# Third convolution of a four-layer block, written out image by image, with a smaller-of-two similarity in place of a squared-norm product

## The reference, cut to what matters

```python
EPS = 1e-08
xf = x.reshape(b, c, p)                                   # p = 256 places of an image
dots = einsum('bcp,bcq->bpq', xf, xf)
norms = sqrt(sum(xf * xf, axis=1))
denom = maximum(norms[:, :, None] * norms[:, None, :], EPS)
sim = square(relu(dots / denom))
tx = einsum('oc,bcq->boq', W, xf) + bias[None, :, None]
out = einsum('bpq,boq->bop', sim, tx)
```

## Time and profile before

| | |
|---|---|
| median of 3 runs | 1095.7 us (1092.54 to 1098.52) |
| the profiled execution | 1098.47 us, with a span of 1096.7 us |
| busy, share of the span | PE 81%, DVE 52%, ACT 40%, POOL 35% |
| mean granted PE clock | 0.823 of full |
| third convolution | from about 578 us to about 680.7 us |

### The profile page before, as it was taken

How to read it: one execution, slowest core, us unless ns; L and a number is a source line. 1 busy time by engine, 2 the same in 40 slices (tenths; PEclk the granted TensorE clock), 3 DMA queues, 4 the chain that set the end, 5 groups by cost and what they waited for, 6 DMA issues and landing times.

```text
span 1096.7 us, 16813 instructions
## 1 busy us (share of the span) xinstructions
PE 888.8 (81%) x5406; PEld 412.6 (38%) x5406; DVE 574.0 (52%) x1939; ACT 443.7 (40%) x800; POOL 379.8 (35%) x453
## 2 busy tenths in 40 slices
PE   4867777896888988887778877889999988668895
PEld 1222222221555656553225655223333324442221
DVE  6787764543444444534656555356464456344542
ACT  3212114653345454443442223234343334656552
POOL 0343433555323222243440020543534422014532
PEclk9787777998589798895895666899999995788977
DMA  9400002222000000001340000322223200002421
GB/s 180 65 18 8 7 9 80 79 91 66 1 2 2 2 2 2 2 2 59 107 147 0 0 0 16 121 73 85 80 81 91 80 1 0 0 1 78 130 78 66
DMA packets 48629, 52.43 MB, mean 48 GB/s; under 512 B 18774, under 2 KB 27114, under 8 KB 48554
## 3 DMA queue, kind: packets, MB, share of 16 engines
q1 hardware_dynamic: 47530, 50.43, 16.9%
q0 software_dynamic: 1024, 1.05, 0.5%
HBM read 49.75 MB, written 1.70 MB: 47 GB/s over the span
## 4 chain that ended last, share of the span: by engine, by line
PE 60%; DVE 17%; issue 9%; POOL 7%; ACT 4%; DMA 1%; SPq 1%; DVEq 1%; POOLq 0%; ACTq 0%
PE ps L772 16%; PE ps L777 10%; PE ps L1260 5%; PE ps L327 4%; PE ps L1305 3%; PE ps L1613 2%; PE ps L1255 2%; DVE code L475 2%; DVE best L471 2%; PE ps L1232 2%; PE ps L1595 2%; POOL work L1140 2%; PE ps L1586 1%; PE ps L714 1%; POOL frstd L1085 1%
## 5 line engine op out<-in xcount | busy, mean ns | idle before, releaser
L772 PE MATMUL ps<-xT,wall 64*128 64x512 f32 x576 | 172.3, 680 | 7.0 <-ACT work L891 3.3
L777 PE MATMUL ps<-work,down 128*64 128x512 f32 x576 | 164.1, 650 | 9.0 <-POOL work L1128 8.3
L1007 DVE TENSOR_TENSOR work<-aq,ps 128x512 f32<-128x512 f32 x128 | 82.2, 684 | 106.9 <-PE ps L772 105.6
L891 ACT ACTIVATE work<-ps,b1t 128x512 f32<-128x512 f32 x160 | 100.4, 685 | 79.7 <-PE ps L772 79.5
L1121 POOL TENSOR_TENSOR work<-xT,cwb 128x512 f32<-128x512 f32 x64 | 81.4, 1274 | 125.2 <-PE ps L772 97.4
L886 ACT ACTIVATE aq<-ps 128x512 f32<-128x512 f32 x128 | 69.4, 594 | 123.8 <-PE ps L772 123.8
L1140 POOL TENSOR_TENSOR work<-work 128x512 f32<-128x512 f32 x56 | 71.1, 1269 | 87.4 <-DVE work L1033 85.1
L772 PEld LDWEIGHTS ps<-xT,wall 64*128 64x128 f32 x576 | 54.0, 204 | 112.0 <-issue 106.2
L1033 DVE SCALAR_TENSOR_TENSOR work<-ps,b1t,cwb 128x512 f32<-128x512 f32 x64 | 47.9, 748 | 82.8 <-PE ps L777 68.5
L772 PE MATMUL ps<-work,wall 64*128 64x512 f32 x256 | 74.2, 656 | 11.8 <-POOL work L1121 6.5
L777 PEld LDWEIGHTS ps<-work,down 128*64 128x64 f32 x576 | 30.0, 140 | 98.0 <-issue 39.0
(11 more groups left out here) (229 smaller groups left out, 1541.8 us busy)
## 6 DMA issues: line engine op xcount, KB each, us to landing
cwb<-weight_rows SPq DMA_DIRECT2D x320, 128.0 KB, 3.0
wall<-in_L_ffn_w_dram SPq DMA_DIRECT2D x4, 512.0 KB, 10.5
wall<-in_L_ffn_W_dram SPq DMA_DIRECT2D x4, 256.0 KB, 9.5
out_dram<-tokens SPq DMA_DIRECT2D x8, 128.0 KB, 1.7
tokens<-in_x_dram SPq DMA_DIRECT2D x1, 896.0 KB, 5.6
ak<-in_L_conv_emb_dram SPq DMA_DIRECT2D x2, 256.0 KB
down<-in_L_ffn_W_dram SPq DMA_DIRECT2D x2, 256.0 KB
down<-in_L_ffn_w_dram SPq DMA_DIRECT2D x1, 512.0 KB
```

What stands on the lines that cost most here:

```text
L772: ins = pe.matmul(m.ps[:, bank + half, :], m.wall[r, at + g * P:at + (g + 1) * P], x[r, :], start=True, stop=True)
L777: ins = pe.matmul(m.ps[half * C:half * C + C, bank, :], m.down[l][:, n % G, :], m.hid[:, n % 3, half, :], start=start, stop=True, skip_gro ...
L891: act.activation(m.hid[:, n % 3, half, :], m.ps[:, 2 * (n % 2) + half, :], ACT.Gelu, bias=bias)\
L1007: dve.tensor_tensor(m.hid[:, n % 3, half, :], m.silu[:, n % 2, half, :], m.ps[:, 2 + half, :], ALU.mult)\
```

## The change

The loop over pairs becomes slots over images, all written out, in which PE handles image j+2 (transposes), j+1 (dot products), j (linear map) and j-1 (outputs). The norm moves from DVE to POOL, and every token is normed twice there: by the layer norm's deviation, and to unit length (64 times the variance, at least 1e-30, to the power -1/2). Both versions stand side by side in a 128-channel tile, so that one transpose turns both. PE makes two sets of dot products from the two halves of the rows; ACT scales the plain ones by 1e8 and takes relu, DVE takes the smaller of that and the cosine, bounded below by zero, and ACT squares it. This is the same value as the quotient with the floor EPS. The ones product, the diagonal, the squared norms and the products with the inverses are gone. The bias is loaded spread over the partitions (`m.lb`) and added by DVE. Statistics of four images and the norms of two now come at the end of the second feed-forward.

```diff
-    ld(m.nat[0:C, 6, C:C + 1], d.L2_conv_bias.rearrange("(o a) -> o a", a=1), s.ld_small)
+    ld(m.lb[:, :], d.L2_conv_bias.partition_broadcast(P), s.ld_small)
...
-            c2_stats(dve, m, s, 0)
+            for i in range(4):
+                c2_stats(dve, m, s, i)
...
-        c2_inverse(pool, m, s, 0)
+        c2_norm(pool, m, s, 0)
+        c2_norm(pool, m, s, 1)
...
+def c2_norm(pool, m, s, i):
+    o = m.pool_order
+    k = 2 * (i % 4)
+    wait_apart(pool, m, s.c2_mv, i + 1)
+    pool.tensor_scalar(m.veps[:, 0:2], m.mv[:, k:k + 2, 1], 1e-6, 1.0, ALU.add, ALU.mult)
+    o.then(pool.tensor_scalar(m.veps[:, 2:4], m.mv[:, k:k + 2, 1], float(C), 1e-30, ALU.mult, ALU.max))
+    pool.tensor_tensor(m.rstd[:, 0:4], m.veps[:, 0:4], m.minus_half[:, 0:4], ALU.pow)
+    o.then(pool.tensor_tensor(m.xc[:, 0:2, :], m.X[:, 2 * i:2 * i + 2, :], bcast(m.mv[:, k:k + 2, 0:1], [P, 2, C]),
+                              ALU.subtract))
+    if i >= 2:
+        pool.wait_ge(s.c2_nt, i - 1)
+    for a in range(2):
+        ins = pool.tensor_tensor(m.an[:, i % 2, :, a, :], m.xc[:, 0:2, :],
+                                 bcast(m.rstd[:, 2 * a:2 * a + 2].unsqueeze(2), [P, 2, C]), ALU.mult)
+    ins.then_inc(s.c2_xn, 1)
...
+def c2_slots(steps, also):
+    for j in range(-3, IMAGES + 2):
+        for step, lead in steps:
+            if 0 <= j + lead < IMAGES:
+                step(j + lead)
+        also(j)
...
+    def dots(i):                                   # PE
+        pe.wait_ge(s.c2_xf, i + 1)
+        if i > 1:
+            pe.wait_ge(s.c2_least, i - 1)
+        x = m.features[:, i % 4, :]
+        for k in range(2):
+            for a in range(2):
+                r = slice(a * C, a * C + C)
+                ins = pe.matmul(m.ps[:, 2 + 2 * (i % 2) + a, k * PLACES:(k + 1) * PLACES], x[r, k * P:(k + 1) * P], x[r, :],
+                                 start=True, stop=True)
+        ins.then_inc(s.c2_dots, 1)
...
+    c2_slots([(tokens, 2), (dots, 1), (linear, 0), (outputs, -1)], also)    # PE; router steps at j = 9, 10, 14
+    c2_slots([(bounds, 0), (features, 2), (squares, 0)], also)              # ACT; router steps at j = 9, 12, 14
+    c2_slots([(least, 0), (linear, 0), (add, -1), (stats, 5)], also)        # DVE; router steps at j = 5, 6, 11, 12, 13
+    c2_slots([(norm, 3)], also)                                             # POOL; router steps at j = 7, 8
...
+    def least(i):                                  # DVE
+        dve.scalar_tensor_tensor(m.least[:, i % 2, :], m.ps[:, 3 + 2 * (i % 2), :], 0.0, m.relu[:, i % 2, :],
+                                 ALU.max, ALU.min).then_inc(s.c2_least, 1)
```

More of the change, by code:

```diff
@@ new lines, in c2_stats @@
+def c2_stats(dve, m, s, i):
+    o = m.dve_order
+    k = 2 * (i % 4)
+    for t in range(2):
+        ins = dve.bn_stats(m.stats[:, k + t, :], m.X[:, 2 * i + t, :])
+    o.then_apart(ins, m)
+    for t in range(2):
+        ins = dve.bn_aggr(m.mv[:, k + t, :], m.stats[:, k + t, :])
+    ins.then_inc(s.c2_mv, 1)
+def c2_norm(pool, m, s, i):
+    o = m.pool_order
+    k = 2 * (i % 4)
+    wait_apart(pool, m, s.c2_mv, i + 1)
[10 more added lines that the diff above has]
+    ins.then_inc(s.c2_xn, 1)
@@ L1602, in turn, with outputs @@
                             start=True, stop=True)
         ins.then_inc(s.c2_lin, 1)
[L1604 to L1615, removed]
+    def outputs(i):
+        pe.wait_ge(s.c2_sq, i + 1)
+        pe.wait_ge(s.c2_tx, i + 1)
+        if i > 0:
+            pe.wait_ge(s.c2_added, i)
+        for t in range(2):
+            for k in range(2):
+                ins = pe.matmul(m.ps[:, 6, t * C:(t + 1) * C], m.sim[:, i % 2, k, t * P:(t + 1) * P],
+                                m.tx[:, 2 * (i % 2) + k, :], start=(k == 0), stop=(k == 1))
@@ L1663, in c2_stats @@
-def c2_stats(dve, m, s, p):
-    ln_stats(dve, m.dve_order, m, m.X[:, bass.ds(p * PT, PT), :], PT, s.c2_mv)
-def c2_dve(dve, nc, m, s):
[L1668 to L1719, removed]
-    router_stats, router_moments, rank, hits, combine = ffn_dve_routing(dve, m, s, 2)
[L1721 to L1729, removed]
@@ L1732, in c2_inverse, with also @@
-def c2_inverse(pool, m, s, p):
-    wait_apart(pool, m, s.c2_mv, p + 1)
-    ln_rstd(pool, m.pool_order, m, PT, 1e-6, s.c2_rstd)
-def c2_pool(pool, nc, m, s):
[L1738 to L1750, removed]
+    def also(j):
+        if j == 9:
+            turn_tokens(0)
+        elif j == 10:
+            router_logits(0)
+        elif j == 14:
+            turn_weights(0)
@@ new lines, in c2_pe, with features, bounds, squares @@
+    c2_slots([(tokens, 2), (dots, 1), (linear, 0), (outputs, -1)], also)
+def c2_act(act, nc, m, s):
+    def features(i):
+        act.wait_ge(s.c2_nt, i + 1)
+        if i >= 4:
+            act.wait_ge(s.c2_lin, i - 3)
+        act.activation(m.features[:, i % 4, :], m.ps[:, 0, 0:PLACES], ACT.Copy).then_inc(s.c2_xf, 1)
+    def bounds(i):
+        act.wait_ge(s.c2_dots, i + 1)
+        if i > 1:
+            act.wait_ge(s.c2_least, i - 1)
+        act.activation(m.relu[:, i % 2, :], m.ps[:, 2 + 2 * (i % 2), :], ACT.Relu, scale=1e8).then_inc(s.c2_relu, 1)
+    def squares(i):
+        act.wait_ge(s.c2_least, i + 1)
+        if i > 1:
+            act.wait_ge(s.c2_y, i - 1)
+        act.activation(m.sim[:, i % 2, :, :].rearrange("p k q -> p (k q)"), m.least[:, i % 2, :], ACT.Square)\
+            .then_inc(s.c2_sq, 1)
+    turn_tokens, router_exps, turn_weights = ffn_act_routing(act, m, s, 2)
+    def also(j):
+        if j == 9:
+            turn_tokens(0)
+        elif j == 12:
+            router_exps(0)
+        elif j == 14:
+            turn_weights(0)
+    c2_slots([(bounds, 0), (features, 2), (squares, 0)], also)
@@ new lines, in c2_dve, with stats, linear, add @@
+def c2_dve(dve, nc, m, s):
+    def stats(i):
+        if i >= 4:
+            dve.wait_ge(s.c2_xn, i - 3)
+            c2_stats(dve, m, s, i)
+    def least(i):
+        dve.wait_ge(s.c2_dots, i + 1)
+        dve.wait_ge(s.c2_relu, i + 1)
+        if i > 1:
+            dve.wait_ge(s.c2_sq, i - 1)
+        dve.scalar_tensor_tensor(m.least[:, i % 2, :], m.ps[:, 3 + 2 * (i % 2), :], 0.0, m.relu[:, i % 2, :],
+                                 ALU.max, ALU.min).then_inc(s.c2_least, 1)
+    def linear(i):
+        dve.wait_ge(s.c2_lin, i + 1)
+        if i > 1:
+            dve.wait_ge(s.c2_y, i - 1)
+        dve.tensor_tensor(m.tx[:, 2 * (i % 2):2 * (i % 2) + 2, :], m.ps[:, 1, 0:2 * C].rearrange("p (t c) -> p t c", c=C),
+                          bcast(m.lb[:, :].unsqueeze(1), [P, 2, C]), ALU.add).then_inc(s.c2_tx, 1)
+    def add(i):
+        dve.wait_ge(s.c2_y, i + 1)
+        x = m.X[:, 2 * i:2 * i + 2, :]
+        dve.tensor_tensor(x, x, m.ps[:, 6, 0:2 * C].rearrange("p (t c) -> p t c", c=C), ALU.add).then_inc(s.c2_added, 1)
+    router_stats, router_moments, rank, hits, combine = ffn_dve_routing(dve, m, s, 2)
+    def also(j):
+        if j == 5:
+            dve.wait_ge(s.c2_added, 4)
+            router_stats(0)
+        elif j == 6:
+            router_moments(0)
+        elif j == 11:
+            rank(0)
+        elif j == 12:
+            hits(0)
+        elif j == 13:
+            combine(0)
+    c2_slots([(least, 0), (linear, 0), (add, -1), (stats, 5)], also)
@@ L1762, with norm, also @@
+def c2_pool(pool, nc, m, s):
+    def norm(i):
+        if i >= 2:
+            c2_norm(pool, m, s, i)
+    scale, centre, norm_tokens = ffn_pool_norm(pool, m, s, 2)
+    def also(j):
+        if j == 7:
+            scale(0)
+        elif j == 8:
+            centre(0)
+            norm_tokens(0)
+    c2_slots([(norm, 3)], also)
 DOTS3 = ((3, 4), (6, 1))
@@ L2134, in program @@
         m.pb = sb("pb", [P, C])
+        m.lb = sb("lb", [P, C])
         m.nat1 = sb("nat1", [C, 3, 2, C])
```

84 lines of the change are left out of this document (18 added, 66 removed), and 2 rows, old and new, of the table SEMS.

## The result

| | before | after |
|---|---|---|
| median of this comparison | 1094.12 us (1091.95 to 1098.52, 4 runs) | 1054.66 us (1052.65 to 1059.87, 4 runs) |
| profiled execution, and its span | 1098.47, 1096.7 | 1053.21, 1051.4 |
| mean granted PE clock | 0.823 | 0.845 |
| third convolution, its first work behind the barrier to the next part's first product | 102.7 us | 63.3 us |

The ratio is 0.9636, with a 95% interval of 0.9605 to 0.9667. Forecast was 1053.

A forecast was written before the change was run, and what follows sets the result against it. PE was taken to bound the third convolution at 1.2 GHz, a serial DVE chain at 2.4 GHz. Part saves 38.8 us, next feed-forward 3.9: 1098.47 less 42.7 gives 1055.8, less 2.8 to the median, 1053; range 1040 to 1078.

The forecast's parts named there:

- That the new part keeps PE at 2.4 GHz for most of the time: Third convolution: PE at 2.4 GHz 76% of the time, so 3.28 us an image and 52.5 for 16.
- The slot: PE's time per image in the third convolution: 5.12 us at 1.2 GHz, 2.95 at 2.4 GHz.
- the 0.37 us that the prediction had left over: Dot products: 2.08 us for eight records against 1.71 streaming, the rest read as agreeing with a tiling-mode drain; nothing added.
- POOL: POOL's norms in the third convolution: 2.7 to 2.8 us per image, just under PE's 3.28.
- The router's norm: POOL's 4.2 us step between two images' norms; half taken as seen by PE, 2.0 us, bounds 0 and 4.2.
- rival (c): POOL or DVE bounds the part at 2.4 GHz, slot 4.0 us instead of 3.28; 1064 us, chance 0.15.
- DVE at slots 11 to 13: Ranking, hits and combining, 5.6 us on DVE, fall in these slots; 3 us reach PE, bounds 0 and 4.
- The mean clock: Granted PE clock over the third convolution, taken as 0.88 from the second convolution, which has the same form.
- Start and end: Barrier opens near 580.3, 1.0 us extra before first dots; next feed-forward saves 3.9 us, its rows landed by the barrier.
- (a): Rival for the third convolution: PE always at 2.4 GHz, 52.4 us saved, 1043 us; chance 0.14.
- (b): Rival for the third convolution: clock down throughout, as in the old part, 1079 us; chance 0.12.
- (d): Rival: the dots' row halves don't overlap, 3.71 us an image at 1.2 GHz, slower at 1105 us; chance 0.03.

The follow-up runs named there:

- e1_serial: Changed kernel with each image's dot products, linear map and outputs made in one slot on PE; 1099.35 us, ratio 1.0022 to the kernel before.
- e10_serial_filled: e1_serial plus three unread products of ones per image where PE waits for the square, one DVE wait moved ahead; 1069.55 us, ratio 0.976.
- e7_old_filled: Kernel before the change plus one unread 512-column product of ones per turn, ahead of the wait for the diagonal; 1084.82 us, ratio 0.9891.
- e2_rows_apart: Changed kernel with both dot products of one row half made before those of the other, instead of in turn; 1050.86 us, ratio 0.9606.
- e4_late_weights: Changed kernel with the router's weights turned in slot 17 instead of 14; 1066.02 us, ratio 0.9739 to the kernel before.
- e3_ones_back: Changed kernel plus one unread 256-column product of ones per image, ahead of its outputs; 1046.16 us, ratio 0.9567 to the kernel before.
- e6_filled: Changed kernel plus unread products: two before the barrier; 1, 4, 3 and 1 before outputs of images 6 to 9; 1045.57 us, ratio 0.9535.
- e8_best: Changed kernel plus unread products: two before the barrier, one per image before its outputs, two for images 7 and 8; 1048.39 us, ratio 0.9553.
- e5_centre_on_dve: Changed kernel with the subtraction of the mean moved from POOL to DVE, behind the statistics; 1060.16 us, ratio 0.9682 to the kernel before.

## Why the prediction was right

**That the new part keeps PE at 2.4 GHz for most of the time** was the main step. It held in the first profile (a clock of 0.82 is 64% of the part at 2.4 GHz) and not in the second (0.67, 34%). That the clock matters is shown: `e1_serial` has all of the new arithmetic and gains nothing, at a clock of 0.53; `e10_serial_filled` wins back 29.8 us with useless products. But the clock isn't the whole gain. `e7_old_filled` has the old part at 0.80 and gains a quarter; one execution of `e2_rows_apart` has the new one at 0.56 and still has the part done 20 us sooner, mostly because PE no longer waits for DVE. The prediction had only 11% from this at 1.2 GHz, the work saved on PE, 1.24 us a pair or about 10 us over the part.

**The slot.** At 1.2 GHz 5.07 measured against 5.12, with two errors that cancel: outputs 1.90 and not 1.66, the linear map 0.74 and not 0.95. At 2.4 GHz 2.71 against 2.95: the linear map in the stream takes 0.38 us and not 0.55, and the dots 1.06 and not 1.14, since in the timeline a group's length reaches over the start of the next one. For the same reason the 0.37 us that the prediction had left over isn't a cost of changing between full and half rows. It sets the 2.08 of the timeline against 1.71 of the chain of waits, and the timeline gives 2.07 for the very ones product that the chain has at 1.71. The Trainium skill says that changing the tiling mode drains the engine (TensorEngine Tiling (Array Packing), Key Properties). No run here shows what that costs; with the changes in every slot the dots are still 2.08 us in the timeline, as in the earlier trace rows.

**POOL** was placed "only just" under PE. With the true 2.71 it lies above, at 2.88, so at 2.4 GHz rival (c) holds in kind, while its price (a slot of 4.0) doesn't. The router's norm cost PE 2.09 + 1.63 = 3.7 us, where 2.0 were taken, near the upper bound of 4.2, and it was followed by 13.7 us at 1.2 GHz (39.6 in the second profile), which the sum had only as part of a mean.

**DVE at slots 11 to 13** was put at 3.0 us. PE waits 0.39 and 0.18 us for DVE itself there, and 1.17 for the last image's square, which is behind DVE's late steps. Part of these slots ran at 1.2 GHz, where the lower bound of 0 applies.

**The mean clock** was taken as 0.88 from the second convolution and was 0.82 in this execution, 0.67 in another. This is the term that was mis-sized. In the first profile it was offset by the shorter slot and by DVE: 63.3 us from the first transposes against 61.6. In the second it wasn't, and the part took 70.5; the total still came to 1058.71, as the remainder was 5.3 us shorter there than in the first. That the median of 1054.66 lies within 2 us of 1053 is partly luck.

**Start and end.** From POOL's last product to the first transposes 5.9 us, as forecast; up to the first dots 1.9 more. At the next part's first products 3.3 us are saved against 3.9, and the first down product comes 8.3 us after the first up product, before 14.1, though over the whole remainder the difference is 4.0 in this pair. `e4_late_weights` confirms the cause, the turning of the weights at slot 14. But the rows had not landed by the barrier, as the prediction had them: POOL still waits 1.09 us for them behind it.

**The rivals.** (a), always up, came near only with unread products added, in `e3_ones_back` and `e6_filled` at 1046, with 0.95. (b) showed in one execution of `e2_rows_apart`. (d) is refuted by the dots at 2.0 us.

**Open:** why the clock, once down, comes up again after 6.8 us in one execution and not for 39.6 in another, with PE busy nearly all the time in both. `e8_best` shows that a filling doesn't settle it. Whether PE or the build brings the row halves together in `e2_rows_apart` is open too.

## What to carry to other kernels

Read the granted clock by windows before counting a matrix engine's work: a serial chain in each turn may cost through the clock as well as through the wait, and putting different images' steps side by side lessened both here. A few unread products in a gap are a cheap probe for this; where they make the kernel faster, the clock is what is being paid for. Look for one-off steps between two slots, here the router's norm: the clock fell behind it in five profiles, and relieving POOL in every slot (`e5_centre_on_dve`) didn't prevent it. Splitting that step wasn't tried. And profile one kernel more than once before splitting its gain among causes.

## What the runs showed of the hardware

- More work on PE made three kernels faster: medians of 1099.35 to 1069.55, 1095.06 to 1084.82, 1054.66 to 1046.16 us, with ratios to the kernel before of 1.0022 to 0.976, 1 to 0.9891, 0.9636 to 0.9567.
- PE busy 97% over 81 us stayed at 0.56 of the clock, while 0.95 was granted to a kernel with PE busy 94% of 58.9 us. At 1.2 GHz the same products take about twice as long (eight records of an image's dots 2.01 us and 1.06), which by itself raises the share, so the share doesn't tell the level.
- One and the same kernel had this part in 63.3 us at a clock of 0.82 and in 70.5 at 0.67, with total times of 1053.21 and 1058.71 us in those executions. The clock fell at the same place in both, behind a wait of PE for POOL, and stayed down for 13.7 and 39.6 us.
- Products on the two halves of the rows overlap in whichever order the program gives them: eight records of 64x256 in 2.01 to 2.02 us of the chain of waits at 1.2 GHz, where eight on one half took 3.71.
